# Self-attention units of a Perceiver block: masked keys spread over three engines, sums by TensorE, output divided in place of probabilities, values of both batches in one product

## The reference

```python
xq, xk, xv = (x @ w.T).reshape(B, T, 32, 16)   # for wq, wk, wv
xq, xk = rotary_pos_emb(xq), rotary_pos_emb(xk)
scores = jnp.einsum('bqhd,bkhd->bhqk', xq, xk) * 16 ** -0.5
scores = jnp.where(causal, scores, -1e30)
probs = softmax(scores, axis=-1)
out = jnp.einsum('bhqk,bkhd->bqhd', probs, xv).reshape(B, T, 512)
return out @ wo.T
```

## Time and profile before

| | |
|---|---|
| median of 3 runs | 2840.89 us |
| the profiled execution | 2835.77 us |
| its span | 2834.0 us |
| TensorE busy in the span | 2631.8 us, 93% |
| VectorE, ScalarE, GpSimd busy | 68%, 54%, 53% |
| stage `sa2`, from its first instruction to the first transposes of `sa3` | 2642.2 to about 2737.8 us of the span |
| mean granted TensorE clock | 0.96 of full |

### The profile page before, as it was taken

The page is one execution under the profiler, slowest core; times in us unless marked ns, Lnnn a source line. Parts: engine busy times, 40 slices in busy tenths (PEclk is TensorE's granted clock), DMA queues, the critical chain, the costliest instruction groups (busy, mean ns, idle before and its releaser), DMA issues. The chain is left out here.

```text
span 2834.0 us, 43610 instructions
## 1 busy us (share of the span) xinstructions
PE 2631.8 (93%) x17320; PEld 2410.2 (85%) x17320; DVE 1917.5 (68%) x2192; ACT 1524.1 (54%) x2702; POOL 1493.7 (53%) x1021
## 2 busy tenths in 40 slices
PE   7999999999999999999999999998867877997878
PEld 6899999999999999999999999997754445775667
DVE  2266776777667767766776677665559997786773
ACT  3455665566556656655665566554344442663552
POOL 2344754655555573574474475430029961794752
PEclk9999999999999999999999999999978998998879
DMA  5410110110111011011111010005230003331100
GB/s 202 135 46 23 61 48 29 54 54 31 34 58 39 25 52 61 23 54 46 38 47 54 23 61 25 29 34 191 73 125 30 1 15 119 127 131 46 49 1 15
DMA packets 90415, 163.81 MB, mean 58 GB/s; under 512 B 8114, under 2 KB 57522, under 8 KB 87658
## 3 DMA queue, kind: packets, MB, share of 16 engines
q1 hardware_dynamic: 81898, 152.70, 16.1%
q10 hardware_dynamic: 8320, 8.39, 0.9%
HBM read 143.17 MB, written 17.89 MB: 57 GB/s over the span
## 5 line engine op out<-in xcount | busy, mean ns | idle before, releaser
L357 POOL TENSOR_TENSOR xa_pt_lo<-xa_st,xa_pt_hi 128x1024 fp32r<-128x1024 f32 x255 | 510.3, 2035 | 596.1 <-ACT xa_pt_hi L543 596.1
L54 PE MATMUL xa_kv_ps<-ctx_wv_hi,ctx_hi 128*128 128x256 f32 (+1 forms) x1664 | 467.6, 281 | 3.1 <-DVE xa_v_lo L634 3.1
L56 PE MATMUL xa_kv_ps<-ctx_wv_hi,ctx_lo 128*128 128x256 f32 (+1 forms) x1664 | 469.7, 282 | 0.0
L55 PE MATMUL xa_kv_ps<-ctx_wv_lo,ctx_hi 128*128 128x256 f32 (+1 forms) x1664 | 465.4, 280 | 0.0
L54 PE MATMUL xa_kv_ps<-ctx_hi,ctx_wk_hi 128*128 128x402 f32 (+1 forms) x1024 | 356.4, 348 | 2.4 <-DVEq L711 2.2
L56 PE MATMUL xa_kv_ps<-ctx_hi,ctx_wk_lo 128*128 128x402 f32 (+1 forms) x1024 | 353.1, 345 | 0.0
L55 PE MATMUL xa_kv_ps<-ctx_lo,ctx_wk_hi 128*128 128x402 f32 (+1 forms) x1024 | 352.8, 344 | 0.0
L634 DVE TENSOR_TENSOR xa_v_lo<-xa_kv_ps,xa_v_hi 128x512 fp32r<-128x512 f32 (+1 forms) x224 | 146.2, 653 | 265.8 <-ACT xa_v_hi L516 264.7
L54 PEld LDWEIGHTS xa_kv_ps<-ctx_wv_hi,ctx_hi 128*128 128x128 f32 (+1 forms) x1664 | 306.4, 184 | 3.3 <-DVE xa_v_lo L634 3.3
L55 PEld LDWEIGHTS xa_kv_ps<-ctx_wv_lo,ctx_hi 128*128 128x128 f32 (+1 forms) x1664 | 308.5, 185 | 0.0
L56 PEld LDWEIGHTS xa_kv_ps<-ctx_wv_hi,ctx_lo 128*128 128x128 f32 (+1 forms) x1664 | 306.7, 184 | 0.0
(11 more groups left out here) (416 smaller groups left out, 7085.6 us busy)
## 6 DMA issues: line engine op xcount, KB each, us to landing
ca_nat<-in_ctx SPq DMA_DIRECT2D x48, 512.0 KB, 3.7
ctx_raw<-in_ctx_t SPq DMA_DIRECT2D x24, 804.0 KB, 6.7
ctx_wk_raw<-in_xa_wk SPq DMA_DIRECT2D x64, 256.0 KB, 2.8
ctx_wv_raw<-in_xa_wv SPq DMA_DIRECT2D x32, 512.0 KB, 4.4
q_raw<-in_xa_wq SPq DMA_DIRECT2D x8, 1024.0 KB, 4.9
q_scratch<-q_q_sb ACTq DMA_DIRECT2D x8, 1024.0 KB, 4.4
xa_q_raw<-q_scratch SPq DMA_DIRECT2D x64, 128.0 KB, 2.6
o_scratch<-xa_o_sb SPq DMA_DIRECT2D x64, 128.0 KB, 1.7
```

Of the source, the lines that this page charges most:

```text
L54: nc.tensor.matmul(out, left[0], right[0], start=first, stop=False)
L55: nc.tensor.matmul(out, left[0], right[1], start=False, stop=False)
L56: return nc.tensor.matmul(out, left[1], right[0], start=False, stop=last)
L357: nc.gpsimd.tensor_tensor(by_chunk(pt_lo, p), scored(j, p).rearrange("p g q c -> p g c q"), by_chunk(pt_hi, p).bitcast(F32), ALU.subtract) ...
```

## The change

Four edits of `sa2`, and one that follows from them in `sa3`:

1. The masked keys of a unit are made by three engines. ScalarE writes heads 0 to 3 of `kb_hi` (four activations of 128x128 with the mask column as scale), GpSimd heads 4 to 7 of `kb_hi` and heads 0 to 3 of `kb_lo` (four instructions of 128x256), VectorE heads 4 to 7 of `kb_lo` (two of 128x256).
2. The exponentials no longer give a sum. `values` makes the sums by TensorE, from the transposed probabilities and a 128x2 matrix of ones (`head_sum`).
3. The probabilities are not divided. The multiplication on GpSimd and its hand-over are gone: `attend` waits for the exponentials. The output of each unit is multiplied by the reciprocals in VectorE's copy to `o_sb`.
4. `values` multiplies both batches at once: 128 weight columns (both batches) by 64 columns (v of both batches), of which only the two matching blocks are used. `o_ps` becomes four buffers of one unit each, and `o_sb` is laid out with 128 partitions.

The split of wo moves from the start of ScalarE's program to units 3 to 6, in four pieces; its low part moves to units 4 to 7; the zeroing of `rest` moves behind GpSimd's second unit. VectorE's loop is now blocks(n+1), softmax(n), low(n-2), output(n-3).

```diff
@@ buffers and semaphores
-        o_sb = top.sb("o_sb", [L, B, H])
+        o_sb = top.sb("o_sb", [P, RT, H])
-            nmx, sm, rs_ = sc.sb("nmx", [P, 2, HC]), sc.sb("sm", [P, 2, HC]), sc.sb("rs", [P, 2, HC])
+            nmx, rden = sc.sb("nmx", [P, 2, HC]), sc.sb("rden", [P, 2, HC])
+            head_sum = sc.sb("head_sum", [P, HP], F32R)
+            NO = 4
-            o_ps = sc.ps("o_ps", [L, 2, BR, 512])
+            o_ps = sc.ps("o_ps", [P, NO, 512])
@@ masked keys
-            def blocks(eng, out, kt, n, sem):
+            def blocks(eng, out, kt, n, a):
+
                 for b in range(BR):
-                    end = eng.tensor_tensor(out[:, n % 2, b], kt[:, r, c, b * L:(b + 1) * L].bitcast(F32).unsqueeze(1)
-                                            .broadcast_to([P, HC, L]), wide(hm[:, :]), ALU.mult)
-                end.then_inc(sem, 1)
+                    end = eng.tensor_tensor(out[:, n % 2, b, a:a + HA], of_batches(kt, n)[:, b].unsqueeze(1)
+                                            .broadcast_to([P, HA, L]),
+                                            hm[:, a:a + HA].unsqueeze(2).broadcast_to([P, HA, L]), ALU.mult)
+                return end
@@ GpSimd
-                    if n > 0:
-                        m = n - 1
-                        pool.wait_ge(r_set, m + 1)
-                        nc.gpsimd.tensor_tensor(s_sb[:, m % NS], s_sb[:, m % NS], wide(rs_[:, m % 2, :]),
-                                                ALU.mult).then_inc(p_set, 1)
...
+                for n in range(NU):
+                    if n >= 2:
+                        pool.wait_ge(s_full, n - 1)
+                    blocks(nc.gpsimd, kb_hi, kt_hi, n, HA)
+                    blocks(nc.gpsimd, kb_lo, kt_lo, n, 0).then_inc(kb_pool, 1)
+                    if n == 0:
+                        nc.gpsimd.memset(head_sum[:, :].bitcast(F32), 0.0).then_inc(sum_zero, 1)
...
+                    if n == 1:
+                        weights.zero(nc.gpsimd)
+                    if 4 <= n < 4 + KC:
+                        k = n - 4
@@ TensorE
-                    pe.wait_ge(kb_hi_set, n + 1)
-                    pe.wait_ge(kb_lo_set, n + 1)
+                    pe.wait_ge(kb_act, n + 1)
+                    pe.wait_ge(kb_pool, n + 1)
+                    pe.wait_ge(kb_dve, n + 1)
...
-                    pe.wait_ge(p_set, n + 1)
+                    pe.wait_ge(e_set, n + 1)
...
-                    for b in range(BR):
-                        for i in range(HC // HP):
-                            cs = slice(c * P + i * HP * HD, c * P + (i + 1) * HP * HD)
-                            ls = slice(b * L, (b + 1) * L)
-                            end = product(nc, o_ps[:, r % 2, b, cs], (pt_hi[:, n % 2, i, ls], pt_lo[:, n % 2, i, ls]),
-                                          (v_hi[:, r * BR + b, cs], v_lo[:, r * BR + b, cs]), True, True)
+                    both = slice(r * BR, (r + 1) * BR)
+                    out = o_ps[:, n % NO, 0:BR * P].rearrange("p (b d) -> p b d", b=BR)
+                    for i in range(HC // HP):
+                        os = slice(i * HP * HD, (i + 1) * HP * HD)
+                        cs = slice(c * P + i * HP * HD, c * P + (i + 1) * HP * HD)
+                        product(nc, out[:, :, os], (pt_hi[:, n % 2, i, :], pt_lo[:, n % 2, i, :]),
+                                (v_hi[:, both, cs], v_lo[:, both, cs]), True, True)
+                        total = o_ps[:, n % NO, BR * P + i * HP:BR * P + (i + 1) * HP]
+                        nc.tensor.matmul(total, pt_hi[:, n % 2, i, :], head_sum[:, :], start=True, stop=False)
+                        end = nc.tensor.matmul(total, pt_lo[:, n % 2, i, :], head_sum[:, :], start=False, stop=True)
@@ ScalarE
-                act.wait_ge(wo_in, 16)
-                nc.scalar.activation(wo_hi[:, :, :], wo_raw[:, :, :], ACT.Copy).then_inc(wo_hi_set, 1)
+                def masked(n):
+
+                    if n >= 2:
+                        act.wait_ge(s_full, n - 1)
+                    for h in range(HA):
+                        end = nc.scalar.activation(kb_hi[:, n % 2, :, h, :], of_batches(kt_hi, n), ACT.Copy,
+                                                   scale=hm[:, h:h + 1])
+                    end.then_inc(kb_act, 1)
+
+                masked(0)
                 for n in range(NU):
+                    if n + 1 < NU:
+                        masked(n + 1)
                     act.wait_ge(d_set, n + 1)
                     for h in range(HC):
                         s = s_sb[:, n % NS, h, :]
-                        end = nc.scalar.activation(s, s, ACT.Exp, bias=nmx[:, n % 2, h:h + 1],
-                                                   accum_out=sm[:, n % 2, h:h + 1])
+                        end = nc.scalar.activation(s, s, ACT.Exp, bias=nmx[:, n % 2, h:h + 1])
                     end.then_inc(e_set, 1)
                     if n > 0:
                         high(act, n - 1)
+                    if 3 <= n < 3 + KC:
+                        act.wait_ge(wo_in, 16)
+                        nc.scalar.activation(wo_hi[:, n - 3, :], wo_raw[:, n - 3, :], ACT.Copy).then_inc(wo_hi_set, 1)
@@ VectorE
-                def output(r):
-                    dve.wait_ge(o_full, (r + 1) * KC)
-                    nc.vector.tensor_copy(o_sb[:, r * BR:(r + 1) * BR, :], o_ps[:, r % 2]).then_inc(o_free, 1)
+                def output(n):
+
+                    r, c = units[n]
+                    dve.wait_ge(o_full, n + 1)
+                    nc.vector.reciprocal(rden[:, n % 2, :], o_ps[:, n % NO, BR * P:BR * P + HC]).then_inc(rden_set, 1)
+                    dve.wait_ge(rden_set, n + 1)
+                    for b in range(BR):
+                        ls = slice(b * L, (b + 1) * L)
+                        end = nc.vector.tensor_tensor(
+                            o_sb[ls, r, c * P:(c + 1) * P].rearrange("p (h d) -> p h d", d=HD),
+                            o_ps[ls, n % NO, b * P:(b + 1) * P].rearrange("p (h d) -> p h d", d=HD),
+                            rden[ls, n % 2, :].unsqueeze(2).broadcast_to([L, HC, HD]), ALU.mult)
+                    end.then_inc(o_free, 1)
@@ sa3
-                        for b in range(BR):
-                            o = k * P + b * L
-                            end = nc.tensor.transpose(t_ps[:, r, o:o + L], o_sb[:, r * BR + b, k * P:(k + 1) * P],
-                                                      ident[0:L, 0:L])
+                        ks = slice(k * P, (k + 1) * P)
+                        end = nc.tensor.transpose(t_ps[:, r, ks], o_sb[:, r, ks], ident[:, :])
```

More of the change, by code:

```diff
@@ L2591, in _ @@
             def _(pool):
[L2592 to L2606 removed]
+                for n in range(NU):
[5 more added lines that the diff above has]
+                        nc.gpsimd.memset(head_sum[:, :].bitcast(F32), 0.0).then_inc(sum_zero, 1)
+                        pool.wait_ge(sum_zero, 1)
+                        for h in range(HP):
+                            nc.gpsimd.memset(head_sum[h * L:(h + 1) * L, h:h + 1].bitcast(F32), 1.0).then_inc(sum_ones, 1)
+                        pool.wait_ge(sum_ones, HP)
+                    if n == 1:
+                        weights.zero(nc.gpsimd)
+                    if 4 <= n < 4 + KC:
+                        k = n - 4
+                        pool.wait_ge(wo_hi_set, k + 1)
                         nc.gpsimd.tensor_tensor(wo_lo[:, k, :], wo_raw[:, k, :], wo_hi[:, k, :].bitcast(F32),
@@ L2697, in softmax @@
                     nc.vector.tensor_reduce(nmx[:, n % 2, :], s, AX_X, ALU.max, negate=True).then_inc(d_set, 1)
-                def sums(n):
-                    dve.wait_ge(e_set, n + 1)
-                    nc.vector.reciprocal(rs_[:, n % 2, :], sm[:, n % 2, :]).then_inc(r_set, 1)
                 def low(n):
@@ L2717, in _ @@
                             dve.wait_ge(s_full, n)
-                        blocks(nc.vector, kb_lo, kt_lo, n + 1, kb_lo_set)
+                        blocks(nc.vector, kb_lo, kt_lo, n + 1, HA).then_inc(kb_dve, 1)
                     if n < NU:
                         softmax(n)
-                    if n > KC and n % KC == 2 % KC:
-                        output(n // KC - 1)
-                    if 1 <= n <= NU:
-                        sums(n - 1)
-                    if n >= 2:
+                    if 2 <= n:
                         low(n - 2)
-                output(RT - 1)
+                    if n >= 3:
+                        output(n - 3)
+                output(NU - 1)
                 weights.scales(dve, s_ps[:, NU % 2, :])
```

30 lines of the change are left out of this document (12 added, 18 removed).

## The result

| | before | after |
|---|---|---|
| median of the runs (of one chip) | 2838.69 us (4 runs) | 2860.81 us (2858.20 to 2863.49, 4 runs) |
| ratio, 95% interval | | 1.0082 [1.0068, 1.0097] |
| span of the profiled execution | 2834.0 us | 2855.8 us |
| stage, first masked keys to the next stage's first transposes | 2642.19 to 2737.82, 95.6 us | 2643.06 to 2760.20, 117.1 us |
| mean granted clock in the stage | 0.71 | 0.69 |

The change made the kernel 0.8% slower: 22 us, where I had forecast 4.8 us less than before (2836.1) and a range up to 2853. The spans differ by 21.8 us and the stages by 21.5, so next to nothing outside the stage took part.

The account below looks back on a forecast made before the run. VectorE was taken to bound units at full clock, TensorE at half. The start (1.5) and units (6.8) gave -8.3 us, the end even, clock falls +3.5: -4.8, so 2836.1 us, range 2826 to 2853.

Parts of the forecast that it names:

- start to scores 3: Start of the stage: scores 3 at about 2656.4 against 2657.87, 1.5 us earlier.
- scores 4 to 8 (quarters of wo): Middle units of 4.2 us; ScalarE's quarters of wo in units 3 to 6 add 0.2 each, 0.8 together.
- the other eight units: Remaining units between scores 3 and 15: 4.2 us each at full clock, plus 3.2 for the magnitudes.
- 3.5 for the clock: Middle units: three falls of TensorE's clock expected, 3.5 us together, from 0 to 15.
- from scores 15 on: End of the stage: about 14.5 us with the same fall of the clock, against 14.8 before; counted as even.
- the one of GpSimd: GpSimd in the units: 3.0 us, 4.7 with wo's low part in units 4 to 7; nothing waits.
- the clock stays down: Rival, TensorE's units: half clock persists, each such unit 3.6 us more; at 8 units +20 us, 2861; chance 0.17.
- The magnitudes: ScalarE, units 10 to 13: about 4.8 us of magnitudes ahead of masked keys, 3.2 us of it delaying scores.
- The full-clock unit: TensorE's middle unit at full clock: scores, transposes, values and sums together 4.1 to 4.2 us.
- the sum matmul: TensorE, 8 added small matmuls per unit: 0.111 us each, 0.89 together at full clock, 1.7 at half.
- the sums hide: Rival, TensorE's units: the 8 small matmuls cost 0.48 us, a unit 3.8; -10.4 us, 2830.5; chance 0.2.
- VectorE and GpSimd still collide: Rival, masked keys: GpSimd holds VectorE's to 1.9 us, VectorE's unit is 4.5; -1 us, 2840; chance 0.15.

Follow-up runs that it names:

- e7: On e1: two columns of ones behind each 32 columns of v replace the sum matmuls, and the magnitudes move to the last units; 2829.79 us.
- e9: On e7: the low parts of wo return to units 4 to 7 of GpSimd; 2843.96 us.
- e1: On the changed kernel: the four low parts of wo on GpSimd move two units later, to units 6 to 9; 2851.54 us.
- e3: On e1: each pair of sum matmuls is issued twice, 8 more small matmuls in each unit; 2877.01 us.
- e5: On e1: each sum matmul streams 64 columns in place of 2, with number, weights and order kept; 2844.22 us.
- e10: On e7: the value products stream 2 x 56 columns in place of 2 x 34, with number and weights kept; 2825.83 us.
- e12: On the kernel before: the value products stream 64 columns in place of 32, with weights, number and order kept; 2833.77 us.
- e8: On e1: the four magnitudes move to the last units and behind the last `high` copy; 2839.94 us.

## Why the prediction was wrong

The stage was to get 4.8 us shorter and got 21.5 longer, an error of 26.3. By the steps of the forecast, from the starts of the scores:

| step | forecast | measured | error |
|---|---|---|---|
| start to scores 3, against before | -1.5 | 15.9 against 15.7: +0.2 | +1.7 |
| scores 4 to 8 (quarters of wo) | 4 x 4.2 + 0.8 = 17.6 | 35.3 | +17.7 |
| the other eight units | 36.8 and 3.5 for the clock | 43.7 | +3.4 |
| from scores 15 on, against before | even | 22.2 against 18.8: +3.4 | +3.4 |

**The step that failed** is the one of GpSimd: "the low part of wo in units 4 to 7 makes these 4.7, but it works up to a unit ahead. Nothing waits." I had costed the work, and the wait that the diff itself added, `pool.wait_ge(wo_hi_set, k + 1)` in place of `(wo_hi_set, 1)`, at nothing, without asking what stands ahead of the quarter on ScalarE. It is `high`, which waits for transposes, which stand behind scores. GpSimd waited 27.0 us in four waits, and the scores came 8.6 to 9.0 us apart in place of 4.2. To work ahead is worth nothing where the thing waited for is made by the unit in hand. Put back alone into e7, where TensorE has room, the wait costs 14 us (e9); taken out of the changed kernel it gives 8 to 11 (e1: 7.6 in the medians, 11.4 between scores 4 and 8 of one execution), since there the clock stays low. The 17.7 of the table are both: 7.2 us of idle time in front of the four scores, and the rest TensorE's work at a mean clock of 0.60.

**The clock.** My rival "the clock stays down" gave 2861, and 2860.8 was measured. That the numbers meet is luck: I had it at 8 units of half clock by themselves, and in the trace four of them are the loop's. It is what is left behind the loop, though. e1's profiled execution, with no wait, holds 0.65; the sums, correctly priced at 0.11 and 0.21, fill TensorE with work during which the clock was low (e3: 0.64), and with more streamed by the same instructions it was higher (e5, e10, e12). I had counted 3.5 us for falls. The tail shows it too: the last two values of the changed kernel take 4.27 us each at half clock (from 2747.84 to 2752.11), those of the kernel before took 2.66 (from 2728.21 to 2730.87). That is 3.2 of the 3.4 us, which I had counted as even.

The Trainium skill ("TensorE: Matmul & The Clock Gate", section "What's actually happening") says that the default state is throttled and activity releases the throttle. The traces agree in that the clock fell over idle time (full before the gap of 3.62 us in e9, 0.50 behind it), and disagree if activity is read as "busy in the profile": in e1's last values TensorE was busy for 20.00 of 20 us at 0.50. In the prediction I set that rule against the rival, beside the row at 0.50 with TensorE nearly always busy, which spoke the other way; the rival deserved more than 0.17.

**The magnitudes** were the right mechanism with the wrong size: 3.2 us forecast, 9.3 to 11.8 measured (e7, e8). The changed kernel's own trace has 6.9 us of it in the four units. The forecast had any fall of the clock behind them only as a share of its 3.5 us.

**The start.** Scores 3 were to come 14.2 us behind the first masked keys and came 15.9 behind. TensorE's and ScalarE's timelines:

```profile
2653.65 0.80 PE L54 MATMUL sa_s_ps<-sa_kb_hi,of_tern 128*128 128x512 f32 x1 [2.74 <-ACT sa_kb_hi L2690]
...
2656.37 0.77 PE L2640 MATMUL sa_t_ps<-all_ident,sa_s_sb 128*128 128x128 f32 x4
...
2657.18 0.60 ACT L2680 ACTIVATE sa_pt_hi<-sa_t_ps 128x512 fp32r<-128x512 f32 x1 [1.67 <-PE sa_t_ps L2640]
...
2657.67 1.26 ACT L2690 ACTIVATE sa_kb_hi<-sa_kt_hi,sa_hm 128x128 fp32r<-128x128 f32 x4
```

The forecast gave scores 2, transposes 0 and `high` 2.7 us together, a price for full clock. They took 4.0, since scores 2 ran 2.72 us at half clock behind a gap of 2.74. That is 1.3 of the 1.7 us of error. A small slip in the sum, too: the unit at half clock has 2.66 us for the values where the same paragraph prices them at 2.56. With that it is 7.7 us, and e1 shows 7.67.

**What held.** The full-clock unit (4.06), the sum matmul (0.111 and 0.213; "the sums hide" is out), eight exponentials in 2.0 us, masked keys of ScalarE 1.26, GpSimd's 2.4 to 2.7, and VectorE, which never bounds (62.8 us of work in 117; "VectorE and GpSimd still collide" is out).

Not separated: what "values of both batches in one product" does by itself. How the clock chooses between its levels is not settled either: e1's six executions spread over 17 us with one and the same program.

## What to carry to other kernels

When an edit makes a wait finer (piece k for the whole), follow the piece to the engine that makes it and up that engine's queue: if anything there waits for the unit in hand, the consumer's lead is gone, and a loop shows as a period that doesn't change when you take work away. Side work (a split, magnitudes) belongs behind what the next unit needs, or in the tail. And where small matmuls with many weight columns fill TensorE at half clock, join them rather than add more (ones beside v: 12.4 us on e1, 9.9 on e8). Letting them carry more columns cost nothing here, and is worth a trial: 7.2 us (e5), and 4.2 (e10) and 2.3 (e12) that are within the noise.
